# A two-layer decoder on one core: inputs loaded a stage ahead, eight scatters a tile instead of seven, divided gathers

## The reference

```python
x = _layernorm(x + _L0_attn_ref(x, ...))             # "self": differential causal attention, 32 q heads, 8 kv heads
x = _layernorm(x + _L0_xattn_ref(x, ctx, ctx, ...))  # "cross": 16 heads of 16, keys and values from ctx_1024
x = _layernorm(x + _L0_ffn_ref(x, ...))              # "moee": one shared expert and top 2 of 8 routed experts
x = _layernorm(x + _L1_attn_ref(x, ...))             # "ssm": Mamba-2 like state space, 8 heads, state 128
x = _layernorm(x + _L1_xattn_ref(x, ctx, ctx, ...))  # "causal": 16 heads, causal mask, keys and values from ctx
x = _layernorm(x + _L1_ffn_ref(x, ...))              # "ffn": relu MLP 256-1024-256 with two LoRA experts, summed
```

```python
shared = silu(xt @ sg_w.T) * (xt @ su_w.T) @ sd_w.T
topk_p, topk_idx = top_k(sigmoid(xt @ router_w.T + routing_bias), 2)   # then normalized to sum 1
h = silu(einsum('th,eih->tei', xt, wg)) * einsum('th,eih->tei', xt, wu)
routed = einsum('te,teh->th', w, einsum('tei,ehi->teh', h, wd))
```

## Time and profile before

| | us |
|---|---|
| median of 3 runs | 2823.53 (2819.08 to 2826.96) |
| profiled execution | 2839.41 |
| its span, first to last instruction | 2837.7 |
| mean granted clock of PE in it | 0.930 of full speed |

### The profile page before, as it was taken

The page is one execution under the profiler, slowest core; times in us unless marked ns, Lnnn a source line. Parts: engine busy times, 40 slices in busy tenths (PEclk is TensorE's granted clock), DMA queues, the critical chain, the costliest instruction groups (busy, mean ns, idle before and its releaser), DMA issues. The chain is left out here.

```text
span 2837.7 us, 66306 instructions
## 1 busy us (share of the span) xinstructions
PE 2462.3 (87%) x24760; PEld 2028.4 (71%) x24760; DVE 1910.4 (67%) x3087; ACT 1432.2 (50%) x2244; POOL 1565.4 (55%) x1856
## 2 busy tenths in 40 slices
PE   4999999999499997888999994888994899986998
PEld 3676666676366764787999993777774677765997
DVE  2566666677268786263888885999983477774665
ACT  2565565565156664322656563565561455552332
POOL 3566565665335553045666665777664477762343
PEclk7899999999689999799999997999996899997999
DMA  7565555652377873223666663111001777742111
GB/s 163 129 153 141 123 141 130 135 140 59 104 198 195 215 186 88 91 78 138 212 232 217 227 215 117 34 46 46 20 12 48 205 206 204 206 112 78 45 55 49
DMA packets 235833, 368.28 MB, mean 130 GB/s; under 512 B 53601, under 2 KB 167009, under 8 KB 228065
## 3 DMA queue, kind: packets, MB, share of 16 engines
q1 hardware_dynamic: 215040, 286.07, 38.1%
q0 software_dynamic: 17376, 78.13, 7.9%
q10 hardware_dynamic: 3200, 1.05, 0.2%
HBM read 236.47 MB, written 137.89 MB: 132 GB/s over the span
## 5 line engine op out<-in xcount | busy, mean ns | idle before, releaser
L1225 ACT ACTIVATE self_probs<-self_score_ps 128x768 f32<-128x768 f32 x256 | 207.4, 810 | 222.3 <-PE self_score_ps L1127 219.2
L1433 POOL TENSOR_SCALAR_AFFINE_SELECT self_probs<-self_probs 128x512 f32<-128x512 f32 x256 | 167.1, 653 | 221.4 <-ACT self_probs L1225 218.8
L1354 DVE TENSOR_REDUCE self_neg_max<-self_max_ps 128x2 f32<-128x256 f32 x256 | 108.2, 423 | 233.3 <-PE self_max_ps L1113 231.7
L1978 DVE TENSOR_TENSOR moee_in_lo<-moee_in_raw,moee_in_hi 128x1024 fp32r<-128x1024 f32 x80 | 168.1, 2102 | 58.0 <-ACT moee_in_hi L1830 43.6
L672 DVE TENSOR_REDUCE cross_neg_max<-cross_max_ps 128x4 f32<-128x1024 f32 x128 | 155.9, 1222 | 70.5 <-PE cross_max_ps L461 68.9
L589 ACT ACTIVATE cross_probs<-cross_score_ps 128x1024 f32<-128x1024 f32 x128 | 131.1, 1024 | 90.3 <-PE cross_score_ps L483 90.0
L1355 DVE TENSOR_REDUCE self_neg_max<-self_max_ps 128x2 f32<-128x512 f32 x256 | 174.6, 682 | 0.0
L2128 POOL TENSOR_TENSOR moee_h_lo<-moee_h,moee_h_hi 128x512 fp32r<-128x512 f32 x78 | 112.4, 1441 | 92.1 <-ACT moee_h_hi L1865 91.3
L3370 POOL TENSOR_TENSOR ffn_g_lo<-ffn_g_full,ffn_g_hi 128x512 fp32r<-128x512 f32 x64 | 82.3, 1286 | 144.4 <-ACT ffn_g_hi L3271 144.4
L1127 PE MATMUL self_score_ps<-self_q_stack,self_k_stack 49*128 49x128 f32 (+1 forms) x1024 | 131.4, 336 | 26.3 <-issue 11.6
L1865 ACT ACTIVATE moee_h_hi<-moee_h 128x512 fp32r<-128x512 f32 x110 | 69.6, 632 | 167.0 <-DVE moee_h L2031 161.0
(11 more groups left out here) (482 smaller groups left out, 9603.8 us busy)
## 6 DMA issues: line engine op xcount, KB each, us to landing
self_q<-self_q_split SPq DMA_DIRECT2D x48, 512.0 KB, 3.2
self_q_raw<-self_q SPq DMA_DIRECT2D x32, 768.0 KB, 7.7
cross_stacks<-cross_qk SPq DMA_DIRECT2D x64, 384.0 KB, 7.1
causal_stacks<-causal_qk SPq DMA_DIRECT2D x64, 384.0 KB, 7.2
moe_y_tiles<-moee_y SPq DMA_DIRECT2D x55, 256.0 KB
x_tiles<-zeros SPq DMA_DIRECT2D x16, 624.0 KB, 4.6
moee_xT<-x_tiles SPq DMA_DIRECT2D x39, 256.0 KB
cross_qk<-cross_k_split SPq DMA_DIRECT2D x16, 512.0 KB
```

The costliest lines, as they stand in the source:

```text
L1225: nc.scalar.activation(probs[g % 4][:, a, :, P:], score_ps[:, :, P:], ACT.Exp, scale=HD ** -0.5).then_inc(prob_ready, 1)
L1433: pool.affine_select(diagonal, diagonal, [[0, 2], [0, 2], [1, P]], ALU.is_ge, zero, base=0, channel_multiplier=-1).then_inc(prob_masked, 1)
L1978: dve.tensor_tensor(half_in(in_lo[p][:], f), half_in(in_raw[p][:], f), half_in(in_hi[p][:].bitcast(F32), f), ALU.subtract).then_inc(inlo_r ...
```

## The change

1. **Loads ahead.** Two tiles, `front` and `back`, outlive the stages. SP issues the cross attention's weights (1 MB) in self's start, the shared expert's weights (1.5 MB) in cross's start, the state space's input weights (1.3 MB) in the experts' start, the causal attention's weights (1 MB) in the state space's start, and all nine inputs of the feed-forward (2.7 MB) in causal's start, each time after the stage's own first loads and ahead of its second batch.
2. **self**: w has a semaphore of its own; x comes right behind w; DVE splits x (lower_x) ahead of the coefficients, wo and v_pad; POOL's fills are divided and don't wait for each other.
3. **cross and causal**: context and x of batch 0 are loaded first; DVE splits the weights at once; POOL splits context 0 ahead of the fills and context 1 right behind them. Cross attention writes its output into an SBUF tile, `x_kept`, instead of DRAM.
4. **experts**: x and the shared weights are there; 8 scatters for each tile.
5. **state space**: ACT's order in even steps, the place of copy_steps, and the gathers of a step in two pairs behind matrices 1 and 3, where they were at the step's end.
6. **feed-forward**: b's terms and the splits of wo and of u of the first batch come after the first transposes; ACT's z of f = 2 comes ahead of g_hi of f = 1; the residual is taken ahead of z1 of f = 1, the moments after g_full of f = 2, their root on POOL at f = 2.

The core of the diff:

```diff
@@ RowNorm
+    def moments(self, dve, st, d):        # the second half of residual(), now called by itself
@@ cross_attention, SP
-            sp.dma_start(w_all[:], weights).then_inc(consts_loaded, 16)
+            sp.dma_start(c_t[0][:], c_rows[0]).then_inc(c_loaded[0], 16)
+            sp.dma_start(x_tok[0][:], x_rows[0]).then_inc(x_loaded[0], 16)
...
-            load(Step(0, -3), 3)
+            ahead(sp)
             sp.wait_ge(zeroed, FILLS)
...
-                    sp.dma_start(o_rows[st.at(-2)], y_out[p2][:]).then_inc(stored[p2], 16)
+                    dst = kept[:, st.at(-2)] if kept else o_rows[st.at(-2)]
+                    sp.dma_start(dst, y_out[p2][:]).then_inc(stored[p2], 16)
@@ DVE
-            dve.wait_ge(consts_loaded, CONSTS * 16)
-            dve.tensor_copy(w_hi[:], w_all[:]).then_inc(w_hi_ready, 1)
+            dve.wait_ge(w_there, 16)
+            dve.tensor_copy(w_hi[:], w_all).then_inc(w_hi_ready, 1)
...
             dve.wait_ge(v_zeroed, 2)
+            dve.wait_ge(consts_loaded, CONSTS * 16)
@@ POOL (its fills and their waits ahead of this are gone)
+            split_context(Step(0, -3))
+            pool.memset(neg_half[:], -0.5).then_inc(zeroed, 1)
+            for stk in stacks:
+                for g in range(PARTS):
+                    pool.memset(stk[:, :, g * PAIRS // PARTS:(g + 1) * PAIRS // PARTS, :].bitcast(F32), 1.0
+                                ).then_inc(zeroed, 1)
+            pool.wait_ge(zeroed, FILLS)
+            split_context(Step(0, -2))
+            pool.wait_ge(consts_loaded, CONSTS * 16)
+            pool.wait_ge(v_zeroed, 2)
...
-                    if i == 0 and st.has(3):
+                    if i == 0 and st.has(3) and st.has(1):
                         split_context(st)
@@ self_attention, SP
-            sp.dma_start(w_all, weights).then_inc(consts_loaded, 16)
+            sp.dma_start(w_all, weights).then_inc(w_loaded, 16)
+            sp.dma_start(x_tok[0][:], x_rows[0]).then_inc(x_loaded[0], 16)
+            sp.dma_start(ident[:], consts["ident"]).then_inc(consts_loaded, 16)
             sp.dma_start(wo_all, w_out).then_inc(consts_loaded, 16)
...
+            ahead(sp)
@@ DVE
-            dve.wait_ge(consts_loaded, 6 * 16)
+            dve.wait_ge(w_loaded, 16)
             dve.tensor_copy(w_hi[:], w_all).then_inc(w_hi_ready, 1)
...
+            lower_x(Step(0, -3))
+            dve.wait_ge(consts_loaded, 5 * 16)
@@ expert_tiles
-        x_tok = m.sb("x_tok", [P, NT, D])
+        x_tok = x_kept[:].rearrange("p b q d -> p (b q) d")
...
-            sp.dma_start(in_raw[0][:], experts_in[0:P, :]).then_inc(raw_loaded, 16)
-            sp.dma_start(out_raw[0][:], experts_out[0:P, :]).then_inc(raw_loaded, 16)
-            for g in range(B // GROUP):
-                sp.dma_start(x_tok[:, g * GROUP * QT:(g + 1) * GROUP * QT, :], xs[g]).then_inc(x_there[g], 16)
+            ahead(sp)
...
-            FIRST, POINTS = 5, 7
+            FIRST, POINTS = 5, 8
...
-                steps = (g, u, (down_done, (t - 1) * PAIRS + f + 1))
-                if f == 1:
-                    steps = (g, u) + steps[1:]
+                steps = (g, u, u, (down_done, (t - 1) * PAIRS + f + 1))
                 for i, (done, value) in enumerate(steps):
-                    n = (t - FIRST) * POINTS - 3 + 3 * f + i
+                    n = (t - FIRST) * POINTS - 4 + 4 * f + i
@@ state_space, SP
-            sp.dma_start(w_all, w_in).then_inc(w_loaded, 16)
...
             sp.dma_start(alog[:], a_log.partition_broadcast(P)).then_inc(loaded, 16)
+            ahead(sp)
@@ ACT, even steps
                     first_tap(n, 1)
+                    if now:
+                        decays(n, 1)
+                        tails(n)
+                        decays(n, 2)
+                        decays(n, 3)
+                    first_tap(n, 2)
                     if real(n + 4):
                         normalize_x(n + 4)
-                    if now:
-                        decays(n, 1)
-                        decays(n, 2)
-                        tails(n)
-                        decays(n, 3)
-                    first_tap(n, 2)
...
+                    copy_steps(n)
                     if late:
                         normalize_y(n - 1)
-                    copy_steps(n)
@@ POOL
                 if now:
                     matrices(pool, n, 1, high_mat_ready)
+                    gather(n + 7, (0,))
                     matrices(pool, n, 3, high_mat_ready)
+                    gather(n + 7, (1,))
...
-                    if real(n + 7):
+                    if not now:
                         gather(n + 7)
@@ lora_feed_forward, PE
                     if f == 1 and st.has(1):
                         transpose_x(st)
-                    if f == 3 and st.has(1):
-                        project_u(st)
+                        if not st.has(0):
+                            terms_of_b()
+                    if f == 3 and st.has(1) and st.has(0):
+                        project_u(st, 1)
+                    if f == 0 and st.has(0) and not st.has(-1):
+                        project_u(st, 0)
@@ ACT (first_z waits for z_done, then writes z0; upper_wo(f) is a quarter of wo's cast)
+                    if st.has(0) and f != 2:
+                        first_z(st, f)
...
+                    if f == 1 and st.has(0):
+                        first_z(st, 2)
+                    if st.has(0):
+                        act.wait_ge(g_ready, st.at(0) * PAIRS + f + 1)
...
+                    if f == 1 and st.has(1) and not st.has(0):
+                        upper_b()
+                        act.wait_ge(given.loaded, given.LOADS * 16)
+                        upper_wo(0)
+                        upper_wo(1)
@@ DVE
+                        if f == 1 and st.has(-1):
+                            norm.residual(dve, st, -1, [y[:, 0:D] for y in y_ps])
                         dve.wait_ge(delta_done, n + 1)
                         dve.tensor_scalar(z1[f % 2][:], z_ps[f][:], 0.0, val[:, 1:2],
...
-                    if f == 1 and st.has(-1):
+                    if f == 1 and st.has(-1) and not st.has(0):
                         norm.residual(dve, st, -1, [y[:, 0:D] for y in y_ps])
+                    if f == 2 and st.has(-1):
+                        norm.moments(dve, st, -1)
```

318 lines of the change are left out of this document (183 added, 135 removed).

## The result

The changed kernel takes 2789.48 us in the median of 4 runs (2782.19 to 2791.09), the kernel before 2822.95 in the median of 4 (2819.08 to 2826.96). The ratio is 0.9876, with a 95% interval of 0.9854 to 0.9899: 33.5 us faster. The forecast was 2753.0 with a range of 2728 to 2787, so the sign is right, the size half of what I said, and the time lies just outside the range. Two later groups of runs, on different chips, gave the changed kernel 0.9879 (0.9862 to 0.9897) and 0.9903 (0.9883 to 0.9924).

The account below looks back on a forecast made before the run. The prediction took TensorE (PE), busy 87% of the span, to bound the kernel, except VectorE in the state-space stage. Nine local terms summed to -70.5 us, taken off the median 2823.53 to give 2753.0, range 2728 to 2787.

Parts of the forecast that it names:

- Term 1: Start of the first attention: earlier split of w and x_lo let PE and POOL start sooner; -5 us (-3 to -6.5).
- Terms 2 and 7: Starts of cross and causal attention: weights already loaded, so splits and stacks come sooner; -8 us each.
- the carry: Cross and causal starts: batch 0's stacks go out earlier and, in cross, the next batch's steps run 8 to 10 us earlier.
- Rival B: Both attention starts: second waits, POOL behind context 1 and the fills; time 2762 us, chance 0.11.
- Term 3: Cross attention to experts: x stays in SBUF, weights are there, PE waits only for small constants; -8 us (-7 to -8.5).
- Term 4: Experts' shared tiles: eight scatters a tile finish the scatters earlier and remove PE's stall; -5.5 us (-8 to 0).
- Term 5: Start of the state-space stage: w's split done before the first sum, shortening the chain to x(0); -3.5 us (0 to -5).
- Term 6: Inside the state-space stage: ScalarE's new order removes PE's wait at e_ps, gathers move; -10 us (-22 to +10).
- rival D: State-space stage: more meetings of DVE and POOL lengthen products, 1.68 us each; 2870 us at 4 a step, chance 0.02.
- rival A: State-space stage gives nothing or takes some, since gathers hold matrix 3; 2763 to 2773, here 2768 us, chance 0.17.
- Terms 8 and 9: Feed-forward: earlier merge and first product at its start, -8.5 us; residual r moved earlier ends PE's stops inside, -14 us.
- rival E: Feed-forward: r is not what PE waits for, the wait stays with g_hi; 2767 us, chance 0.06.

Follow-up runs that it names:

- before again: The kernel before with no edit, profiled in a second execution: span 2819.7 us.
- after again: The changed kernel with no edit, run again on the same chip as the kernel before's second profile: median 2790.55 us, ratio 0.9879 to the kernel before.
- c1_first: The changed kernel with batch 1's x and context loaded ahead of the next stage's weights and SP's wait for fills, both attentions: ratio 0.9886 to the kernel before.

## Why the prediction was wrong in size

By its own steps, with "same chip" for before again against after again:

- **The basis.** I took the trace as typical but for a factor of 0.56%. It had 12.5 us more in the experts, with stops that the other execution of the same kernel, on another chip, doesn't have, and 6 in self. Of the nine terms this broke the fourth.
- **Term 1, self: -5, measured -3.9.** The two steps were right to 0.2 and 0.4 us: projection at 13.10 (12.9 forecast), q_lo at 19.33 (18.9), released by v_pad. Self varies by 12 us between executions of the changed kernel and its variants (725.8 to 737.6), so the sum itself is only roughly confirmed.
- **Terms 2 and 7, the attentions' starts: -16 together, measured -4.5.** The step that failed is "POOL then waits for context 1, which SP now issues behind 1.5 MB of the shared expert's weights": SP issues it behind its own wait for the fills as well, which stands between `ahead` and the body. It is plain in the code that I quoted. POOL split it at 16.1 after the start in cross, and at 18.1 in causal, where I had it land at about 14.3. The sign that I had named for being wrong, k_lo(0) later than 18 us, came in both: 18.04 in cross (19.32 before) and 20.03 in causal (19.74 before). The second step that failed is the carry: the stacks went out at 24.6 (23.7 forecast) and 26.3 (22.3 forecast), 5.4 and 3.6 earlier than before, but the stage gained less than half of that in cross. That PE started at 8.3 and 6.6, where I had 6.2 and 7, was worth little by itself. Rival B (2762) had the place right; c1_first bought back 2 to 4 a stage. The order of the rings, which the prediction cited from the Trainium skill ("DMA: Bandwidth & Descriptors", section "Queues, rings and completion order"), had little part: context 1 came 3.1 us after its issue in cross and 5.1 in causal, where 2.7 MB were ahead, but it was issued only 13.0 us after the start in both.
- **Term 3, experts' start: -8, measured -7.4** (PE's first g product at 13.8 instead of 21.2 after the stage's start).
- **Term 4, scatters: -5.5, measured -1.4.** The step that failed is the tile's length, "I put the tile at 10.9", worked out on a trace with stops: it was 8.6 without them, and 12.0 or 11.7 with them, past the 11.2 that I had named as a sign of being wrong. In the undisturbed kind the chain of 64 scatters is what bounds: 64 x (0.96 + 0.30) = 80.6 of its 83 to 85 us, whatever the number a tile, since it starts 1.1 us after the slots are known (90.2 after the stage's start) and hardly pauses. A longer stall of PE behind it, 9.43, shows only that PE was faster in front of it. On the other chips 8 a tile costs 3 to 6 us of the stage against 7 (574.2 against 577.0 to 579.9, four kernels of one chip).
- **Term 5, start of the state space: -3.5, measured +1.2 to +3.3.** I had the split of w "done before 1725", ahead of the first sum. The diff doesn't move it, so the stretch of POOL's two little instructions, 1.38 and 1.32 us, stayed to the hundredth. And the load of 1 MB that I set against the 1.3 MB saved is issued later, when the gathers run, and costs 1.8.
- **Term 6, inside the state space: -10 (-22 to +10), measured +8** on the same chip, and +5 between the means of the eleven profiles above. The mechanism was named (the gathers and ScalarE's order change how often POOL and DVE meet) and the sum took its sign from the other side, PE's wait of 17.7, of which it booked 1.5 us in each pair. The wait did go, to 5.0, and PE waited for DVE's product instead. It was not what bounded: with DVE at 95% its removal can be worth no more than what DVE is idle, and nearly all of what DVE's instructions get longer by is paid. The excess went from 42.5 to 50.5 and the pairs from 343.6 to 351.6, 8 for 8. This is rival D's mechanism at a small part of the price I gave it, and together with rival A (2768) it should have had far more than 0.19.
- **Terms 8 and 9, the feed-forward: -22.5, measured -20.5.** The start gave 10.4 (first g_full at 15.7 instead of 26.1), 2 more than forecast. The period went from 14.8 to 14.1, worth 10 instead of 14: r was the cause, as argued against the name in the view of waits (rival E fell), but 0.3 to 0.4 of each 0.97 came back as a new wait for ScalarE's z.

The miss on one chip is 42.5 us: 23 in the state space, 11.5 in the attentions, 5 in the experts, 3 in the rest. Terms 2, 5 and 7 ended outside their own bounds, terms 4 and 6 at the unfavourable side of theirs. The bounds of all nine add to -23 on that side, and the prediction set its upper end at -36.5, on the ground that they wouldn't all fall there; five fell on it together. What four of them have in common (2, 4, 5 and 7) is a gain at a seam or a stall that something else stood right behind.
